# The last chunk of a fused two-layer sequence kernel: deltas on TensorE, norm statistics on VectorE, a smaller last group, and another order of every engine

## The reference

```python
x = _layernorm(x + _L0_attn_ref(x, ...))
x = _layernorm(x + _L0_ffn_ref(x, ...))          # x2 below
x = _layernorm(x + _L1_attn_ref(x, W_k, W_v, W_q))   # x3 below
x = _layernorm(x + _L1_ffn_ref(x, W_r, W_k, W_v, mu_r, mu_k))

# _L1_attn_ref: k, v, q = x W; 32 blocks of 8; the scan runs over the 4 rows
def step(S, kvq):
    k_norm = k_t / (jnp.linalg.norm(k_t, axis=-1, keepdims=True) + 1e-06)
    retrieved = jnp.einsum('bnij,bnj->bni', S, k_norm)
    delta = v_t - retrieved
    S_new = jnp.tanh(S + jnp.einsum('bni,bnj->bnij', delta, k_norm))
    Sq = jnp.einsum('bnij,bnj->bni', S_new, q_t).reshape(B_, n)
    out = Sq * jax.nn.silu(Sq)

# _L1_ffn_ref: x_prev is x of the position before
xr = mu_r * x + (1.0 - mu_r) * x_prev;  xk = mu_k * x + (1.0 - mu_k) * x_prev
out = sigmoid(xr @ W_r.T) * (square(relu(xk @ W_k.T)) @ W_v.T)
```

## Time and profile before

| | us |
|---|---|
| median of 3 runs (lowest, highest) | 1143.12 (1143.03, 1143.18) |
| the profiled execution | 1142.22 |
| its span, first to last instruction | 1140.4 |
| last DVE instruction ends, from the span's start | 1137.89 |

### The profile page before, as it was taken

The page is one execution under the profiler, slowest core; times in us unless marked ns, Lnnn a source line. Parts: engine busy times, 40 slices in busy tenths (PEclk is TensorE's granted clock), DMA queues, the critical chain, the costliest instruction groups (busy, mean ns, idle before and its releaser), DMA issues.

```text
span 1140.4 us, 16645 instructions
## 1 busy us (share of the span) xinstructions
PE 1094.0 (96%) x5837; PEld 848.5 (74%) x5837; DVE 947.4 (83%) x1384; ACT 597.8 (52%) x1011; POOL 514.5 (45%) x426
## 2 busy tenths in 40 slices
PE   8999999999999999999999999999999999999476
PEld 4566666688787777788778887877887787878265
DVE  4788888882045998999899889989998998898897
ACT  2345555554446346644755573566557455744535
POOL 1476667775333244423424432344333244136852
PEclk9999999999999999999999999999999999999788
DMA  7346655523521430423133132314232340321001
GB/s 259 110 165 227 220 206 207 230 94 125 171 93 60 144 111 20 148 74 129 57 110 126 59 106 91 134 37 129 74 129 62 109 142 19 114 91 38 0 1 39
DMA packets 45114, 127.01 MB, mean 111 GB/s; under 512 B 4352, under 2 KB 21504, under 8 KB 43136
## 3 DMA queue, kind: packets, MB, share of 16 engines
q1 hardware_dynamic: 43904, 114.20, 30.1%
q10 hardware_dynamic: 1152, 12.07, 2.8%
HBM read 117.86 MB, written 19.92 MB: 121 GB/s over the span
## 4 chain that ended last, share of the span: by engine, by line
PE 75%; DVE 14%; POOL 5%; issue 3%; ACT 2%; DMA 0%; SPq 0%; POOLq 0%; DVEq 0%; ACTq 0%
PE lower L1264 45%; PE bank L1264 17%; PE lower L440 5%; PE lower L572 2%; POOL state L748 2%; POOL rgn L757 2%; PE bank L1253 1%; DVE tmp L2297 1%; PE bank L487 1%; DVE y L847 1%; DVE tmp L2311 1%; DVE Sq L2299 1%; DVE y L852 1%; PE lower L526 1%; DVE tmp L2322 1%
## 5 line engine op out<-in xcount | busy, mean ns | idle before, releaser
L2064 POOL TENSOR_TENSOR a_lo<-whole,a_hi 128x512 fp32r<-128x512 f32 x128 | 181.4, 1435 | 267.4 <-ACT a_hi L1658 174.6
L1264 PE MATMUL lower<-b_hi,ring 128*128 128x512 f32 x512 | 193.6, 396 | 1.4 <-ACT a_hi L1658 1.4
L1264 PE MATMUL lower<-b_lo,ring 128*128 128x512 f32 x512 | 190.7, 390 | 2.4 <-POOL b_lo L2064 2.4
L1264 PE MATMUL lower<-a_hi,ring 128*128 128x512 f32 x496 | 187.4, 394 | 0.0
L1264 PE MATMUL lower<-a_lo,ring 128*128 128x512 f32 x496 | 185.1, 389 | 0.0
L2064 POOL TENSOR_TENSOR b_lo<-whole,b_hi 128x512 fp32r<-128x512 f32 x64 | 93.8, 1474 | 149.2 <-ACT b_hi L1658 125.7
L1641 ACT ACTIVATE S<-S 128x1024 f32<-128x1024 f32 x56 | 58.6, 1059 | 167.0 <-DVE S L2324 167.0
L1657 ACT ACTIVATE whole<-lower,hs 128x512 f32<-128x512 f32 x126 | 86.3, 685 | 85.8 <-PE lower L1264 80.9
L1264 PEld LDWEIGHTS lower<-b_lo,ring 128*128 128x128 f32 x512 | 95.9, 188 | 23.1 <-POOL b_lo L2064 3.4
L1264 PEld LDWEIGHTS lower<-b_hi,ring 128*128 128x128 f32 x512 | 96.2, 188 | 22.0 <-issue 1.8
L440 PE MATMUL lower<-wa,xT 128*128 128x512 f32 x240 | 109.6, 599 | 2.2 <-DVE turned L817 1.4
(11 more groups left out here) (302 smaller groups left out, 2394.0 us busy)
## 6 DMA issues: line engine op xcount, KB each, us to landing
ring<-ffn_copy_dram SPq DMA_DIRECT2D x128, 512.0 KB, 3.4
look<-ffn_dram ACTq DMA_DIRECT2D x6, 1879.0 KB, 6.8
ffn_copy_dram<-ffn_dram SPq DMA_DIRECT2D x4, 2112.0 KB, 10.1
rope<-rope_dram SPq DMA_DIRECT2D x8, 512.0 KB, 8.3
xtok<-x_dram SPq DMA_DIRECT2D x8, 512.0 KB, 3.7
x1in<-x_dram SPq DMA_DIRECT2D x8, 512.0 KB, 4.6
x1res<-x_dram SPq DMA_DIRECT2D x8, 512.0 KB, 3.2
xT<-xT_dram SPq DMA_DIRECT2D x7, 512.0 KB, 8.5
```

Source lines behind the costliest of these rows:

```text
L1264: ins = nc.tensor.matmul(out, a, b, start=(first and n == 0), stop=(last and n == len(pairs) - 1))
L2064: nc.gpsimd.tensor_tensor(lo[:, m, :], t["whole"][:, m % 4, :], hi[:, m, :].bitcast(F32), ALU.subtract).then_inc(lo_done, 1)
```

## The change

The groups of rows for the channel mix are now five, `LEFT`: (6, rows 0-1), (6, rows 2-3), (7, rows 0-1), (7, row 2), (7, row 3), with products with `mixw` for all of them; the results are stored in the order `ENDS`, group 1, 2, 0, 3, 4. For steps one and two of the scan (`BY_TENSOR`) DVE writes state times key into a new tile `times`, with j outermost, so that neighbouring products lie 128 elements (512 bytes) apart; PE adds v and the eight slices, each times the identity, in PSUM, and DVE takes the delta from there. The key is divided by minus its norm, so that the sum of v and the slices is the delta, and the outer product is subtracted. Both outer products are on DVE. The statistics of x3 are all on DVE. The inverse norms are written to PSUM. `mixw` is made in the last `body`, before the first `b_lo` and the first `a_lo`. The 24 unused matmuls are gone. In the last `body`, the wait of `b_lo` for a step of the scan is moved from index 6 to 7.

```diff
+            LEFT = ((LAST - 1, 0, 2), (LAST - 1, 2, BATCH), (LAST, 0, 2), (LAST, 2, 3), (LAST, 3, BATCH))
+            ENDS = (1, 2, 0, 3, FINAL)
+            BY_TENSOR = (1, 2)
-                          (1, 3): read_step(0, 1), (1, 4): read_step(0, 1) + 1, (1, 6): read_step(1, 0),
+                          (1, 3): read_step(0, 1), (1, 4): read_step(0, 1) + 1, (1, 7): read_step(1, 0),
...
+                    def delta(s, hf):
+                        v = kvq[:, s + 1, DIM + hf * cols:DIM + hf * cols + cols]
+                        pe.wait_ge(fin_kv, s + 2)
+                        pe.wait_ge(fin_times_k, step_of(s, hf))
+                        product(tensor_delta(hf), [(ident[:], x) for x in (v, *(t["times"][:, hf, j, :] for j in range(BS)))]
+                                ).then_inc(fin_delta, 1)
...
-                    busy_while_waiting(bank[KEY_BANK[1]], 6)
-                    busy_while_waiting(pair_banks(2)[1], 6)
...
-                        steps.done(nc.gpsimd.tensor_scalar(x, x, 1.0, 1e-6, ALU.mult, ALU.add))
+                        steps.done(nc.gpsimd.tensor_scalar(x, x, -1.0, -1e-6, ALU.mult, ALU.add))
...
+                        if not more and n in (0, KH):
+                            mix_weights(n // KH * 2)
+                            mix_weights(n // KH * 2 + 1)
...
-                    def outer_product(s):
-                        nc.gpsimd.tensor_tensor(last_outer(t), along_i(t["delta"][:, 0:HALF, :]), along_j(k),
-                                                ALU.mult).then_inc(fin_readq, 1)
...
+                    def times_key(s, hf):
+                        k, _, _, st, _, w = last_parts(s + 1, hf)
+                        if s in BY_TENSOR:
+                            w = t["times"][:, hf].rearrange("p j (n i) -> p n i j", i=BS)
+                        dve.wait_ge(fin_post, step_of(s, hf))
+                        keys_scaled(s + 1)
+                        nc.vector.tensor_tensor(w, st, along_j(k), ALU.mult).then_inc(fin_times_k, 1)
+                    def outer(s, hf):
+                        k, _, _, _, dl, w = last_parts(s + 1, hf)
+                        if s in BY_TENSOR:
+                            dl = tensor_delta(hf).rearrange("p (n i) -> p n i", i=BS)
+                            dve.wait_ge(fin_delta, delta_of(s, hf))
+                        done(nc.vector.tensor_tensor(w, along_i(dl), along_j(k), ALU.mult), "outer", s, hf)
+                    def earlier_moments():
+                        moments(ln3, x3, t["mv3"], ve3)
+                    def x3_moments(g):
+                        row_stats(fin, x3, range(rows.start, rows.stop))
+                        row_moments(fin, t["mv3"], rows, ve3)
```

More of the change, by code:

```diff
@@ L1553, in busy_while_waiting @@
[L1553 to L1562 removed]
+                        ins.then_inc(left_dr, 1)
@@ L2606, in moments_of @@
[L2606 to L2615 removed]
+                    def earlier_moments():
+                        moments(ln3, x3, t["mv3"], ve3)
+                        ln3.end()
@@ L2633, in finish @@
+                    outer(0, 0)
+                    outer(0, 1)
                     next_state(0, 0)
```

960 lines of the change are left out of this document (493 added, 467 removed).

## The result

| | before | after |
|---|---|---|
| median of 4 runs (lowest, highest) | 1143.07 (1142.33, 1143.18) | 1132.4 (1131.61, 1134.19) |
| the profiled execution | 1142.22 | 1132.0 |
| its span | 1140.4 | 1130.1 |
| last DVE instruction ends | 1137.89 | 1126.40 |

The changed kernel takes 0.9911 of the time, 95% interval 0.9897 to 0.9925: 10.2 us faster, between 8.6 and 11.8 (the two medians differ by 10.7). The forecast was 1132.8. The total came out at 0.4 us from it, but all four terms were wrong by 0.5 us or more, in both directions, and a cost at the stores was not in the sum at all.

A forecast was written before the change was run, and what follows sets the result against it. DVE was taken to bound the last 70 us. Four stretches gave -11.2, by the queue -11.1; with +0.8 that is -10.3: 1131.9 for the profiled execution, median 1132.8, range 1130.5 to 1135.5 (0.55), 8 in 10 within 1129.0 to 1140.5.

The forecast's parts named there:

- B: PE's deltas come too late, kernel slower: 1164.8 at half clock throughout, mild form 1138.0; chance 0.08, mild 0.06.
- C: Gain is real, but DVE's waits and operations drawn out beside POOL return: gain 6.5, 1136.6; chance 0.13.
- D: No gain at the end: stores or a last body held up by `mixw` take it back; 1143.1; chance 0.08.
- the signs: Trace marks, including DVE's end near 1127 to 1128, products into `times` 1.2 to 1.4 us, POOL's reads 2.3.
- rival A: Strided writes into `times` are slow, four products by +1.2, deltas as late: gain 6.8, 1136.3; chance 0.10.
- First stretch: From the start to the first product of state and key of chunk 7 (old: 1069.41): change 0.0.
- Second stretch: Step zero of the scan and scaling of keys 2 and 3, to the first read sum: 13.2 to 11.5, -1.7.
- Third stretch: From the first read sum to the end of the last read sum: 34.9 to 31.5 us, -3.4.
- extra terms: Added costs: 0.4 for writes at a 512-byte step and 0.4 for overlap of DVE and POOL.
- Tail: From the end of the last read sum to the end of DVE: 20.4 to 14.3 us, -6.1.
- The stores: From the last DVE operation to the end: 2.5 us, left as they are, change 0.
- Just in time: Delta (1,0) from PE at 1086.1, wanted by DVE at 1086.2, no slack; each us of lateness costs a us.

The follow-up runs named there:

- e5: The changed kernel with the deltas of steps one and two made on DVE again, into SBUF: 1142.17, ratio 0.9999.
- e8: The changed kernel with the wait of `b_lo` for a scan step put back from slot (1, 7) to (1, 6): 1133.79, ratio 0.9925.
- e12: The changed kernel with paired `times` layout, group 1's result normed early on ACT, and one POOL read held for DVE's product of (1, 1): 1129.71, ratio 0.9889.
- e10: The changed kernel with the last two rows as one group again and the queue orders rewritten to fit: 1139.62, ratio 0.9975.
- e1: The changed kernel with ACT norming group 1's result earlier, so one store leaves earlier: 1131.8, ratio 0.9900.
- e6: The changed kernel with ten unused matmuls in PE's queue ahead of delta (1, 0), finished 4.2 us later: 1136.21, ratio 0.9951.
- e9: The changed kernel with POOL's four `mix_weights` of the last chunk moved back from the last body into `finish`: 1133.97, ratio 0.9925.
- e4: The changed kernel plus 14 products of 1024 elements at its end, writing or reading at steps of 1 to 128 elements: one run, 1157.44.
- e11: The changed kernel with even and odd j side by side in `times`: DVE writes runs of two, PE reads at 8 bytes: 1130.35, ratio 0.9894.
- e2: The changed kernel with DVE writing `times` in a row and PE reading it at a step of 32 bytes: 1136.45, ratio 0.9945.
- e3: The changed kernel with DVE writing `times` in a row and reading state and key with the step instead: 1133.42, ratio 0.9913.
- e7: The changed kernel with six unused matmuls (12 instructions) put back ahead of `turn_row(1)`: 1132.46, ratio 0.9919.

## Why the prediction was right, and where it wasn't

The forecast's main chain held: DVE was the bound and stayed it, the gain is work and drawn-out time taken from DVE plus waits, and PE brings the deltas in time. Its clock was 1.00 from 1070 in the change; in ten of the twelve other profiles it was 0.66 to 0.83 over 1070 to 1080, but in all of them 1.00 over 1080 to 1090, where the first deltas are made. Rivals B, C and D did not come true. What C rests on, operations drawn out beside POOL, appears in full only with the deltas in SBUF (e5). Of the signs, the products into `times` took 1.9, between the 1.2 to 1.4 of the forecast and the over 2 of rival A, and one read of POOL took 3.77 for 2.3 without delaying DVE.

**First stretch, 0.0 forecast, -1.6 measured.** The step that failed is "DVE now waits for the tanh of state half 0, which ends at 1039.26". I took that time from the old trace for the new kernel; in the new one it ends at 1037.81. The tanh is queued on ACT behind work for PE's hidden products, and these came earlier, since one slot of the table no longer held `b_lo`. e8 brings the old wait back, 2.42, and with it 1.2 to 1.4 us against the profiles at the same clock. The second miss is the wait of 0.8 that the old 1.25 was to become; it did not appear. Against these two stand a first product drawn out to 1.59 and some 0.3 not traced. The -1.6 is also one execution: over the change and the nine kernels that have its first stretch, the first product starts at 1067.45 to 1069.35, which is -2.0 to -0.1, and in six of the nine it is nearer to the forecast than here.

**Second stretch, -1.7 forecast, -2.5 measured.** Mechanism right; the 0.8 put down for a wait on POOL's Newton chain didn't appear, because the inverse at 1077.28 finds it done, by 0.16. All ten of these profiles have 10.66 for this stretch.

**Third stretch, -3.4 forecast (-2.6 with the extra terms), -0.8 measured.** The mis-sized term is the strided writes: +0.1 each forecast, 0.62 to 0.69 each measured from start to start, 2.6 in all. The bounds, 0 to 1.2, held it; I took the end of the nearest row, and the row lay on the other side of a threshold. This is somewhat over half of rival A, whose sums were made with +1.1 each. e12, which takes the writes off and the one overlap, measures 31.6 for the forecast 31.5: the rest of that term was right in sum.

**Tail, -6.1 forecast, -6.6 measured.** Right. e10 shows that the smaller last group carries more of it than I had thought, through the clock too, which the prediction didn't say.

**The stores, 0 forecast, +1.2 measured.** "I leave the 2.5 us as they are" was wrong. In the change 0.9 of it is SP's slow issue. With the last store started at once the remainder is 0.6 in e1 but 1.1 in e12. In both it starts 1.3 behind the fourth, and it lands 2.6 and 3.2 after its start. Why is open; only a part of the 1.2 was had back.

**Just in time.** "With no slack" was 0.5 to 0.6 us in fact (e6). **`mixw`** in the last body costs little there: POOL's first `b_lo` comes at 979.10 against 978.62, 0.5 later where the sum said at most 0.3. Back at the end it costs 1.6 by the ratio, which noise could hide, and 0.9 to 1.7 by the traces (e9).

So the 0.4 between forecast and result is luck in part: errors of 1.6, 0.8 and 0.5 to one side, 1.8 and 1.2 to the other, which leave 0.1 between the forecast for an execution like the profiled one (1131.9) and 1132.0. The rest is that the median stands 0.4 above that execution and not 0.9.

Two parts of the change have no run of their own: the statistics of x3 on DVE, and the inverse norms in PSUM. What they bring is argued from the durations of operations (keys by inverse norm 0.69 for 1.98) and not shown apart.

## What to carry to other kernels

Before you lay data out for another engine, ask which side strides, and keep neighbouring accesses in pairs, at most 8 bytes apart, on both: a pair of elements side by side made the same data free to write for DVE and to read for PE. When an operand can come from PSUM, an operation on DVE is out of POOL's way. In a tail, count what the last row alone must wait for, and look at the clock that TensorE has when that row reaches it; and take an upstream engine's time from the old trace only if none of the edits touches its queue. One profile is one execution: compare the same stretch in several before you say that a clock or a wait costs nothing.

## What was not expected of the hardware

- The price of a step on DVE, fp32, 1024 elements: 1.22 to 1.23 at 4 and 8 bytes, 1.88 to 2.00 from 16 to 512 bytes, for the written and for a read operand alike (e4).
- A moving operand of TensorE of 128 columns pays too: 16 matmuls took 1.95 in a row, 1.98 at a step of 8 bytes, 3.89 at 32 bytes (the change, e11, e2).
- DVE (two SBUF inputs) and the reads of POOL take turns and don't slow each other in part: the later one ends about its own length after the end of the earlier one (DVE 1.08 in e11 and 1.09 in e5, for 1.13 from start to start; POOL 2.1 in the change, for 2.35).
- SP issues a store in 0.34 to 0.40, but in the change and in eight experiments that keep its five stores within some 4 us one of them took 1.13 to 2.01. It was quick in e12, where the first store leaves 4 us ahead of the rest, 0.8 in e1, and also quick (0.44) in e5, which has the burst: what decides it stays open.
- The last store, of 128 KB, took 3.1 to 3.8 from its start to its landing where it started some 0.5 behind the fourth (e2, e3, e5, e6, e9) and 2.3 to 2.4 where it started 1.2 to 2.1 behind it in the change, e4, e7, e8 and e11, one of 256 KB with nothing near it 2.1 (the first of e12).
- The same program in the same stretch had a granted clock of 1.00 over 1050 to 1060 in three profiles and of 0.83 in seven, and the first product of the scan came 30.9 us after the start of the tanh in the three and 31.1 to 31.9 in the seven.
